# Sparse attention with a top-64 search: push-down of found scores by GpSimd in units of 2^60, and the guess update over a ring of four states

## The reference

```
dots = einsum('bhij,hk->bkij', q k^T * scale, pre_proj); causal mask -> neg
vk = top_k(dots, 64)[0][..., -1:]
attn = softmax(where(dots < vk, neg, dots)); attn = einsum('bhij,hk->bkij', attn, post_proj)
```

## Time and profile before

| | us |
|---|---|
| median of 3 runs | 3666.67 (3664.82 to 3668.48) |
| the profiled execution, its own time | 3667.18 |
| its span in the trace | 3665.3 |
| VectorE busy | 3356.8 (92%) |
| ScalarE busy | 3202.9 (87%) |
| TensorE busy | 2800.9 (76%) |
| GpSimd busy | 1432.8 (39%) |

### The profile page before, as it was taken

One profiled execution on the slowest core, in us unless ns is written; L12 is line 12 of the kernel. 1 busy time (PEld: TensorE's weight loads), 2 busy tenths in 40 slices (PEclk: granted clock), 3 DMA queues, 4 the chain that ended last, 5 costly groups with the idle time before them and its releaser, 6 DMA issues. The chain is left out here.

```text
span 3665.3 us, 67866 instructions
## 1 busy us (share of the span) xinstructions
PE 2800.9 (76%) x13751; PEld 1814.3 (49%) x13751; DVE 3356.8 (92%) x13778; ACT 3202.9 (87%) x9018; POOL 1432.8 (39%) x2407
## 2 busy tenths in 40 slices
PE   7777878777767877777777767777777787777755
PEld 3455555555544555555455545554455455445544
DVE  4699999999999999999999999999999999999994
ACT  1799999999978999999999979998999999999973
POOL 3233443343334443444443334343444344343433
PEclk9888898889888989889899888989889889898986
DMA  1000000000000000000000000000000000000000
GB/s 41 7 2 2 4 8 5 8 2 5 8 4 8 5 8 2 5 8 5 8 5 8 2 4 8 5 8 2 5 8 5 8 2 6 6 5 8 2 7 4
DMA packets 31377, 22.38 MB, mean 6 GB/s; under 512 B 3202, under 2 KB 30339, under 8 KB 30723
## 3 DMA queue, kind: packets, MB, share of 16 engines
q1 hardware_dynamic: 30722, 16.03, 1.5%
HBM read 11.83 MB, written 4.19 MB: 4 GB/s over the span
## 5 line engine op out<-in xcount | busy, mean ns | idle before, releaser
L840 ACT ACTIVATE signs<-scores,state 128x528 int8<-128x528 f32 (+3 forms) x3072 | 1764.3, 574 | 200.4 <-DVE state L1122 124.0
L1236 POOL TENSOR_SCALAR probs<-probs,rinv 128x528 f32<-128x528 f32 (+3 forms) x1024 | 546.1, 552 | 1696.0 <-DVE rinv L1022 1694.8
L682 PE MATMUL s_bank<-xn,gT 128*128 128x512 f32 (+3 forms) x2048 | 916.3, 576 | 2.3 <-issue 1.5
L706 PE MATMUL t_bank<-ident,probs 128*128 128x128 f32 x2560 | 477.8, 311 | 283.5 <-POOL probs L1236 275.5
L693 PEld LDWEIGHTS y_bank<-u_all,probsT 128*128 128x128 f32 x5120 | 620.5, 195 | 134.0 <-issue 124.9
L693 PE MATMUL y_bank<-u_all,probsT 128*128 128x128 f32 x5120 | 625.3, 278 | 6.9 <-ACT probsT L851 6.8
L840 ACT ACTIVATION_READ_ACCUMULATOR signs<-scores,state 128x1 f32 x3072 | 576.0, 187 | 0.0
L1017 DVE SCALAR_TENSOR_TENSOR probs<-scores,kth,expo 128x528 f32<-128x528 f32 (+3 forms) x1024 | 522.2, 565 | 31.1 <-issue 23.6
L706 PEld LDWEIGHTS t_bank<-ident,probs 128*128 128x128 f32 x2560 | 299.1, 153 | 485.9 <-issue 380.6
L861 ACT ACTIVATE expo<-scores,negmax 128x528 f32<-128x528 f32 (+3 forms) x1024 | 535.1, 575 | 0.0
L983 DVE TENSOR_SCALAR_CACHE_REDUCE work<-scores,state 128x528 f32<-128x528 f32 (+3 forms) x1024 | 516.1, 559 | 17.8 <-issue 8.1
(11 more groups left out here) (152 smaller groups left out, 3577.7 us busy)
## 6 DMA issues: line engine op xcount, KB each, us to landing
xwork<-in_L_attn_x_dram SPq DMA_DIRECT2D x17, 256.0 KB, 2.8
xres<-in_L_attn_x_dram SPq DMA_DIRECT2D x16, 256.0 KB, 2.9
out_dram<-ybuf SPq DMA_DIRECT2D x16, 256.0 KB, 2.4
u_all<-in_L_attn_Wq_dram SPq DMA_DIRECT2D x1, 512.0 KB, 3.8
u_all<-in_L_attn_Wk_dram SPq DMA_DIRECT2D x1, 512.0 KB, 4.6
u_all<-in_L_attn_Wv_dram SPq DMA_DIRECT2D x1, 512.0 KB, 5.4
u_all<-in_L_attn_Wo_dram SPq DMA_DIRECT2D x1, 512.0 KB
expo<-in_L_ffn_w_gate_dram SPq DMA_DIRECT2D x1, 192.0 KB, 4.8
```

The lines of the kernel that those rows point to most:

```text
L682: nc.tensor.matmul(score_part(t, 0, KEYS[t]), lhsT=gT[s % 2][:, t * P:(t + 1) * P], rhs=xn[par][:, 0:KEYS[t]], start=True, stop=False, ski ...
L706: mm = nc.tensor.transpose(t_bank[q % 2][:, at:at + P], probs[:, h % 2, KEY_AT[t] + j * P:KEY_AT[t] + (j + 1) * P], ident[:, :])
L840: nc.scalar.activation(signs[:, k, 0:ROW[t]], row(scores, ring(head_of(s, k + 1), RING), t), ACT.Sign, bias=state[:, s % 2, S_T, k * T + t ...
L1236: nc.gpsimd.tensor_scalar(prb, prb, rinv[:, slot_p, t:t + 1], 1.0, ALU.mult, ALU.mult).then_inc(scaled, 1)
```

## The change

All scores are kept in units of 2^60: `a_all` and `amem` are multiplied by 2^-60 (`UNIT`) in passes that exist, the seeds by 2^-30 (with the norm, which is now 2^-30 of what it was), Exp gets scale 2^60, `negmax` is made with -2^60, and the mask is -2^40. So every score is tiny beside 1, and "score minus found mark" is the score where the mark is 0, and -1 where it is 1.

- The push-down leaves VectorE. GpSimd does it as four two-input subtracts in place in `work`, one per tile, each as soon as the count of its tile is in (`found_ready`); MAX8 waits for `hidden`.
- The rank table `offset` is made by GpSimd, after the subtracts; the pick waits for `offset_ready`.
- The copy of the guess to `cand` is gone: MAX8 writes its eight values into the state ring behind the guess, so that guess and candidates lie together (`candidates`).
- The guess state is a ring of four, with four parts (guess, miss, other point, its miss). The copy of the last guess is gone, since it is read from the ring; the two products and the two differences are made in one operation each over [128, 2, 12]. 11 operations in place of 14.
- On GpSimd the copy of the memory scores (L1252) moves from the end of the step to right behind the seed copy.

The core of the diff:

```diff
+UNIT = 2.0 ** -60
-MASKED = -2.0 ** 100
+MASKED = -2.0 ** 40
-S_T, S_LAST, S_OTHER, S_PARTS = 0, 1, 3, 5
+S_T, S_MISS, S_OTHER, S_PARTS = 0, 1, 2, 4
+STATES = 4
+PART = (GUESSES + 2) * T + 8 * T
+STATE = S_PARTS * PART
-        state = sb("state", [P, 2, S_PARTS, (GUESSES + 1) * T])
+        state = sb("state", [P, 2 * (STATES - 1) * STATE + PART])
+        def pair(slot, part, k):
+            at = slot * STATE + part * PART
+            return state[:, at:at + 2 * PART].rearrange("p (a c) -> p a c", a=2)[:, :, (k + 1) * T:(k + 1 + GUESSES) * T]
+        def last_and_now(slot):
+            now = slot * STATE + S_MISS * PART + T
+            last = (slot - 1) % STATES * STATE + S_MISS * PART
+            at, step = min(now, last), abs(now - last)
+            both = state[:, at:at + 2 * step].rearrange("p (a c) -> p a c", a=2)[:, :, 0:GUESSES * T]
+            return both, int(last > now)
+        def candidates(slot):
+            at = slot * STATE + S_T * PART + (GUESSES + 1) * T
+            return state[:, at:at + 9 * T].rearrange("p (j t) -> p t j", t=T)
...
                     if selects:
-                        v.tensor_copy(cand[:, :, 0:1].squeeze(2), guessed).then_inc(select_step, 1)
-                        dve.wait_ge(select_step, T)
+                        dve.wait_ge(found_ready, 4 * gk + 4)
                         v.scalar_tensor_tensor(out=spread[:, :], in0=found[:, :], scalar=-2.0 * AIM, in1=found[:, :],
                                                op0=ALU.add, op1=ALU.mult).then_inc(select_step, 1)
-                        v.tensor_tensor(offset[:, :, 0:9], ranks, found[:, :].unsqueeze(2).to_broadcast([P, T, 9]),
-                                        ALU.add).then_inc(select_step, 1)
-                        v.scalar_tensor_tensor(out=work[:, :], in0=work[:, :], scalar=-FMAX,
-                                               in1=scores[:, bass.ds(slot_k, 1), :].squeeze(1),
-                                               op0=ALU.mult, op1=ALU.add).then_inc(select_step, 1)
-                        dve.wait_ge(select_step, T + 2)
+                        dve.wait_ge(select_step, 1)
...
                     def top_scan():
                         if selects:
-                            dve.wait_ge(select_step, T + 4)
+                            dve.wait_ge(hidden, 4 * gk + 4)
+                            alone(dve)
                             for t in ORDER:
-                                v.max(cand[:, t, 1:9], work[:, AT[t]:AT[t] + ROW[t]]).then_inc(select_step, 1)
+                                v.max(candidates(now)[:, t, 1:9], work[:, AT[t]:AT[t] + ROW[t]]).then_inc(select_step, 1)
...
                         v.tensor_tensor(miss, counts[:, :], aim_sum, ALU.subtract).then_inc(guess_step, 1)
+                        v.tensor_tensor(between[:, :, :], pair(past, S_T, -1), pair(now, S_OTHER, 0),
                                         ALU.subtract).then_inc(guess_step, 1)
-                        v.tensor_copy(new[:, S_LAST, T:T + ALL], guess).then_inc(guess_step, 1)
                         dve.wait_ge(guess_step, 1)
-                        v.tensor_tensor(cross[:, :], miss, last, ALU.mult).then_inc(guess_step, 1)
-                        v.tensor_tensor(miss2[:, :], miss, miss, ALU.mult).then_inc(guess_step, 1)
+                        v.tensor_tensor(product[:, :, :], both, miss.unsqueeze(1).to_broadcast([P, 2, ALL]),
+                                        ALU.mult).then_inc(guess_step, 1)
+                        dve.wait_ge(guess_step, 3)
...
+                        v.tensor_tensor(apart[:, :, :], pair(now, S_T, 0), other, ALU.subtract).then_inc(guess_step, 1)
...
+                    if kind != "drain":
...
+                        nc.gpsimd.tensor_copy(mem_parts(scores[:, bass.ds(slot, 1), :].squeeze(1)),
+                                              head_mem(smem[par], s)).then_inc(mem_placed, 1)
+                    if lagged(kind, s, LAG_K):
+                        slot_k = ring(head_of(s, LAG_K), RING)
+                        for p, t in enumerate(ORDER):
+                            pool.wait_ge(found_ready, 4 * (g - LAG_K) + p + 1)
+                            alone(pool)
+                            wrk = work[:, AT[t]:AT[t] + ROW[t]]
+                            nc.gpsimd.tensor_tensor(wrk, row(scores, slot_k, t), wrk, ALU.subtract).then_inc(hidden, 1)
+                    if lagged(kind, s, LAG_K):
+                        at_least(pool, kth_ready, g - LAG_K)
+                        pool.wait_ge(found_ready, 4 * (g - LAG_K) + 4)
+                        alone(pool)
+                        nc.gpsimd.tensor_tensor(offset[:, :, 0:9], ranks, found[:, :].unsqueeze(2).to_broadcast([P, T, 9]),
+                                                ALU.add).then_inc(offset_ready, 1)
                     if lagged(kind, s, LAG_P):
                         gp, slot_p = g - LAG_P, head_of(s, LAG_P) % 2
                         pool.wait_ge(rinv_ready, gp + 1)
```

More of the change, by code:

```diff
@@ L130, in guess_table @@
             active = n + M > TOPK
-            table[i, t] = z
-            table[i, T + t] = z - FAR / (2 * density)
+            table[i, t] = z * UNIT ** 0.5
+            table[i, T + t] = (z - FAR / (2 * density)) * UNIT ** 0.5
             table[i, 5 * T + 9 * T + t] = float(active)
@@ L840, in count @@
                             nc.scalar.activation(signs[:, k, 0:ROW[t]], row(scores, ring(head_of(s, k + 1), RING), t),
[L841 removed]
+                                                 ACT.Sign, bias=guesses(s % STATES, k, GUESSES)[:, t:t + 1], scale=-1.0,
                                                  accum_out=counts[:, k * T + t:k * T + t + 1]
@@ L862, in exponentials @@
                                                  row(scores, ring(head_of(s, LAG_K), RING), t), ACT.Exp,
-                                                 bias=negmax[:, bass.ds(ring(head_of(s, LAG_K), RING), 1), t]
+                                                 bias=negmax[:, bass.ds(ring(head_of(s, LAG_K), RING), 1), t],
+                                                 scale=1.0 / UNIT
                                                  ).then_inc(exp_ready, 1)
@@ L935, in _ @@
             dve.wait_ge(a_taken, 4)
-            nc.vector.tensor_tensor(a_sq[:, :, :], a_all[:, :, :], a_all[:, :, :], ALU.mult).then_inc(squared, 1)
+            nc.vector.scalar_tensor_tensor(out=a_sq[:, :, :], in0=a_all[:, :, :], scalar=1.0 / UNIT, in1=a_all[:, :, :],
+                                           op0=ALU.mult, op1=ALU.mult).then_inc(squared, 1)
             dve.wait_ge(squared, 1)
@@ L979, in step @@
                     moves = any(lagged(kind, s, k + 1) for k in range(GUESSES))
-                    old, new = state[:, s % 2], state[:, (s + 1) % 2]
+                    now, soon, past = s % STATES, (s + 1) % STATES, (s - 1) % STATES
                     def count_found(t):
                         v.tensor_scalar(work[:, AT[t]:AT[t] + ROW[t]], row(scores, slot_k, t), guessed[:, t:t + 1],
-                                        None, ALU.is_ge, ALU.add, accum_out=found[:, t:t + 1]).then_inc(select_step, 1)
+                                        None, ALU.is_ge, ALU.add, accum_out=found[:, t:t + 1]).then_inc(found_ready, 1)
                     if selects:
-                        guessed = old[:, S_T, GUESSES * T:(GUESSES + 1) * T]
+                        guessed = guesses(now, GUESSES, 1)
                         dve.wait_ge(guess_ready, g - 1)
@@ L1090, in step @@
                         alone(dve)
-                        guess, miss, last = old[:, S_T, 0:ALL], new[:, S_LAST + 1, T:T + ALL], old[:, S_LAST + 1, 0:ALL]
-                        other = new[:, S_OTHER:S_OTHER + 2, T:T + ALL]
+                        guess, other = guesses(now, 0, GUESSES), pair(soon, S_OTHER, 1)
+                        miss = pair(now, S_T, 0)[:, 1]
+                        both, last_at = last_and_now(now)
                         v.tensor_tensor(miss, counts[:, :], aim_sum, ALU.subtract).then_inc(guess_step, 1)
-                        v.tensor_tensor(between[:, :, :], old[:, S_LAST:S_LAST + 2, 0:ALL], old[:, S_OTHER:S_OTHER + 2, 0:ALL],
+                        v.tensor_tensor(between[:, :, :], pair(past, S_T, -1), pair(now, S_OTHER, 0),
@@ L1107, in step @@
                                                in1=miss, op0=ALU.is_gt, op1=ALU.mult).then_inc(guess_step, 1)
+                        dve.wait_ge(guess_step, 4)
+                        v.tensor_tensor(other, pair(now, S_OTHER, 0), between[:, :, :], ALU.add).then_inc(guess_step, 1)
                         dve.wait_ge(guess_step, 6)
-                        v.tensor_tensor(other, old[:, S_OTHER:S_OTHER + 2, 0:ALL], between[:, :, :],
-                                        ALU.add).then_inc(guess_step, 1)
@@ L1111, in step @@
-                        dve.wait_ge(guess_step, 8)
-                        v.tensor_tensor(over[:, :], miss, other[:, 1], ALU.subtract).then_inc(guess_step, 1)
```

(9 more changed lines are left out.)

67 lines of the change are left out of this document (36 added, 31 removed).

## The result

The changed kernel takes 3681.16 us (median of 6 runs, 3679.45 to 3681.89), the kernel before 3666.98 beside it (6 runs, 3664.82 to 3669.01): a ratio of 1.0039 (95% interval 1.0027 to 1.0051). It is slower, by 14 us; forecast were 3610 us and a gain.

A forecast was written before the change was run, and what follows sets the result against it. VectorE was taken to set the pace, ScalarE close behind. 1.60 us saved less 1.32 of stall gave 0.28 a step, 72 over 256, three quarters counted: 3667.2 - 55 - 0.5, about 3610 us, range 3515 to 3710.

The forecast's parts named there:

- B: VectorE's stage applying the threshold, four two-input operations; GpSimd's subtracts were to stall it by 1.32 us a step.
- F: VectorE's guess update; going from 14 operations to 11 was to save 0.15 us a step.
- G: VectorE's MAX8 and the two picks; at most 0.04 us a step longer for the nop.
- rival 1: VectorE wins the gaps in B: stall 0.05 us, ScalarE becomes the bound, 3535 us; chance 0.25.
- E: VectorE's select preparation; losing the `cand` copy, rank table's add and push-down was to save 1.49 us a step.
- The sum: VectorE's step: 1.60 us saved less 1.32 of stall, 0.28 a step, 72 over 256, of which 55 counted.
- A: VectorE's first stage in a step, counting the found scores, 2.06 us; claimed not to be slowed by GpSimd.
- Rival 2: In B, the subtracts block for their whole duration: 2.09 us of stall, 3790 us; chance 0.18.
- Rival 3: No difference: VectorE gains 0.28 us, but later `rinv` makes ScalarE wait for transposes; 3665 us; chance 0.07.

The follow-up runs named there:

- experiment 1: Changed kernel with GpSimd's four subtracts cut to the first 8 columns of each tile and MAX8 reading the scores, push-down left out: 3479.07 us.
- experiment 5: Changed kernel with GpSimd's four subtracts replaced by one-input operations over the same columns, MAX8 reading the scores, push-down left out: 3482.13 us.
- experiment 4: Changed kernel with the whole push-down back on VectorE as one subtract of 1344 columns, GpSimd's four subtracts removed: 3632.97 us.
- experiment 8: Changed kernel with only 528 columns subtracted on GpSimd: candidates in their own tile, 3532.85 us; rank-table wait moved ahead of MAX8, 3528.42 us; repeated unchanged, 3528.3 us.
- experiment 2: Changed kernel with VectorE's copies from PSUM moved ahead of its threshold stage: 3576.52 us.
- experiment 7: Changed kernel with GpSimd's four subtracts moved behind the scaling and the `pmem` copy in its queue: 3943.15 us.
- experiment 6: Changed kernel with GpSimd subtracting only the tiles of 528 and 400 columns, VectorE the other 416: 3609.1 us.

## Why the prediction was wrong, point by point

The step that failed is the sum's pair of sizes: the stall that comes back in B, put at 1.32 us a step and measured at 1.49, and the saving in F, put at 0.15 and measured at 0.01. Each alone would have left a gain (0.11 or 0.14 us a step); together, and with G, they turn it into a loss.

- **What bounds the kernel:** right. VectorE led before and leads after. The ceiling behind it was priced too high: rival 1 put the time without any stall at 3535, and experiments 1 and 5 reach 3479 and 3482. I had counted only ScalarE's wait for the guess and a little more; in fact ScalarE's idle time between 150 and 3340 us fell from 273 us in the kernel before to 136 in experiment 1, and of it the wait for transposes from 70 to 36.
- **What comes off E:** 1.49 forecast, 1.50 measured.
- **What comes off F:** 0.15 forecast, 0.01 measured. Experiment 4 splits it: the update with 11 operations is itself 0.09 shorter (2.08 against 2.17), and 0.08 of that is lost in the changed kernel. It is not lost in one place. In both kernels GpSimd's `negmax` stops one of F's first operations, `between` in experiment 4 and `product` in the changed kernel, and there the first five together take some 0.03 more. The changed kernel's two rows, then those of experiment 4:

```profile
L1130 DVE TENSOR_TENSOR product<-state 128x24 f32<-128x24 f32 x258 | 79.2, 307 | 2.6 <-DVE between L1126 2.6
...
L1126 DVE TENSOR_TENSOR between<-state 128x24 f32<-128x24 f32 x258 | 50.7, 196 | 0.3 <-issue 0.3
...
L1128 DVE TENSOR_TENSOR between<-state 128x24 f32<-128x24 f32 x258 | 92.3, 358 | 0.3 <-issue 0.3
...
L1132 DVE TENSOR_TENSOR product<-state 128x24 f32<-128x24 f32 x258 | 46.7, 181 | 0.0
```

  The other 0.06 is in F's last two operations (198 and 315 ns in the mean against 171 and 286). GpSimd's layer-norm passes run beside these in some steps; 61 of the 516 last over 0.25 us, in experiment 4 it is 45. Why more of them are hit no run tests.
- **G:** 0.04 longer forecast, 0.09 measured. The nop and wait in front of MAX8 were priced, the second wait in front of the pick, 0.07 by experiment 8, was not.
- **B against the subtracts:** the mechanism, the turns and which operation is hit were right, and the signs that the prediction named came: the first operation near 0.8 (0.93), the second longer by 0.7 (0.70), the last near 0.55 (0.54). The size was low: 1.32 forecast, 1.49 measured. I took 0.14 us of each hold as hidden in VectorE's own gap; the clean step has stalls of 0.77, 0.49 and 0.22 where the holds were put at 0.83, 0.56 and 0.30, so 0.06 to 0.08 is hidden. That is the error, less the 0.05 at B's start that did not come. In 45 steps the second subtract gets in ahead of B's first operation, which then lasts over 1 us (hence 927 ns in the mean against 767); but the other stalls move up by one operation with it, and B takes 3.5 us in these steps as in the others.
- **The sum:** 0.28 us a step less 0.17 (B), 0.14 (F) and 0.05 (G), plus 0.02 in A, is the 0.06 on the other side. The forecast was a small difference of two large numbers, 1.60 and 1.32, and an error of a tenth in each turned its sign. The distance from -55 to +14 us is within what my bounds allowed, but the chance of 0.72 for a gain was not what such a difference bears.
- **Rival 2** (holds of the full duration, 3790) did not come: 0.77 of 1.03 us. The Trainium skill, SBUF — State Buffer, section SBUF: two separate sides, is right that the loser blocks; here it blocks for the columns and not for GpSimd's fixed 0.2 us. B's first operation shows the same: it runs free although it starts 0.18 us before the subtract of 528 columns ends.
- **Rival 3** (transposes late): ScalarE's wait for them did grow by 100 us, but its wait for the guess fell by 67, and in experiment 2 the kernel is 105 us faster than the changed one although `rinv` comes later still (A + 6.2 in place of 5.65).

## What to carry to other kernels

In this kernel work given to GpSimd was free only beside VectorE's one-input passes (A's pass of 528 columns takes 761 ns before and after) and those from PSUM; against two-input operations its columns cost VectorE more than doing them itself (0.71 us of stall for 400 columns that cost 0.44). So list VectorE's stages by their inputs, find the windows with one input, and hand over only what fits: here one subtract of 1.3 us under stage A, worth 105 us against the same kernel with the push-down on VectorE (3633 to 3528), where all four cost 48. And when a forecast is the difference of two terms many times its size, spend the effort on these two, and give the sign no more certainty than they have.

## What the runs showed of the hardware that was not expected

A tiny VectorE operation pays as much of a GpSimd operation as a large one does: 24 columns took 1.27 us in experiment 7. A waiting GpSimd operation gets its turn between two VectorE passes with accumulators almost every time: in experiment 6 the first or the second operation of B lasts over 1 us in 231 of 256 steps. And a wait for a semaphore that was met long before still costs 0.07 us in a chain of dependent VectorE operations (experiment 8).
